# A fused cross-attention and feed-forward kernel: the eight accumulation banks shared out anew, with new engine orders

## The chip, the core and the metric

The kernel runs on one core of a Trainium2 chip. The metric is the device time in microseconds (us) of one execution. The core has five engines that run side by side and signal each other through semaphores: TensorE (PE) multiplies matrices and writes into PSUM, which has eight banks of 512 fp32 numbers per partition; VectorE (DVE) and ScalarE (ACT) read PSUM and on-chip memory; GpSimd (POOL) works on on-chip memory; SyncE (SP) issues the transfers (DMA).

## The reference

For 64 sequences of 64 rows and 256 columns, with a context of the same shape and a mask, four residual steps are taken (`LN` is a layer norm without weights):

```python
x = x + xattn(LN(x), ctx)      # 8 heads of 8 channels over 256 positions: q, k, v projections, rotary, softmax
x = x + bit_ffn(LN(x))         # activations rounded to 8 bits, ternary weights, hidden 1024, silu(gate) * val
x = x + cross(LN(x), ctx, mask)  # softmax(x ctx^T / 16, masked) ctx
x = x + tern_ffn(x)            # ternary weights by groups of 64, silu(gate) * up, RMS norm, down
```

In the first attention a sequence's 64 channels are the 8 heads of 8 channels each, and its 256 columns are the positions that attend to each other.

## The kernel before

Two sequences make a pair, there are 32 pairs, and a pair has 16 (sequence, head) units. Each unit has a 256 x 256 score matrix, and it is computed twice. **S** (line 435) puts queries on partitions, and DVE takes its row maxima (**mx**, line 871, 512 numbers per partition and unit). The 16 units' maxima are transposed on PE (**mxp**), copied (**mxc**) and written by a transfer (**md**) as an extra row beside the queries, so that the second product **T** (line 443), with keys on partitions, comes out with the maximum already taken off. ACT takes its exponential (**E**, line 591). **pv** (line 457, four per pair) multiplies by the values, and **u** copies the result out. S and T use 31 or 32 rows of PE's 128, a different quarter for each of four units in turn, so that up to four such products can run at once; pv uses 32 columns for each of four units.

All else is a chain of small steps per pair: `proj0 proj1 v` (projections), `r1 pc r2 rot hi lo kq` (rotary and its transfer), `sg rc d1 or ov om y x1` (normalising, output projection), then the first feed-forward network `bsB mvB rsB xnB amB sxB xr xq rq qT`, `Bg Bv` (gate and value products in two halves), `tB aB hB` (tanh on ACT, two products on DVE, each half), `amH sx hr hq ht Bd x2`; then the cross attention `xnD xcT xcTc sc wx pD pT pTc ro x3`; then the second network `xnC xh xl xT Cg Cu th aC hC hh hl hT Cd x4` and the store `st`.

The order of the work is written out by hand in `ORDER`: for each engine a list of steps, `name:shift`. All engines run the same loop of iterations, and in iteration `it` a step works on pair `it + shift`; so eight or more pairs are in flight at once. Each engine runs its list strictly in order and waits at each step for what it needs. Steps of the weight preparation (`c ab ra qa rn cl qb fx tn tc gm gv bs br fr ct val mn`) run once; their shifts are large numbers, which only place them in the first iterations.

PSUM is three tensors: `psS` with two banks for S, `psT` with two for T, `psW` with four for all other products. Unit n of S goes to bank n % 2 and waits until mx has read unit n - 2; T waits in the same way for E. For `psW` the table `BANKS` says which products share a bank, and `turn_before` finds for each product the one that held the bank before it; PE then waits for that one's reader (`READER`: aB1 for Bg1, hC0 for Cu0, aC1 for Cg1, pD for sc and so on). The waits of a step are in the branch of its kind, as here for the score products:

```python
after(pe, "mx", p, n - 2)      # S
after(pe, "E", p, n - 2)       # T
```

`BANK[...]` is used by the readers too (`tc gv r1 pc vst x1 tB aB hB x2 wx pD x3 aC hC x4` and others), so they follow a product to its bank without an edit.

## Time and profile before

| what | value |
|---|---|
| median of 3 runs | 884.59 us (882.81 to 884.67) |
| the profiled execution | 885.19 us, of which the span of instructions is 883.4 us |
| PE busy | 766.2 us, 87% of the span |
| DVE busy | 744.9 us, 84% |
| ACT busy | 688.0 us, 78% |
| POOL busy | 659.1 us, 75% |
| granted clock of PE, mean | 0.947 of full speed |

Busy time is the time in which an engine works on at least one instruction. Products overlap on PE and their ends are modelled, so the distance from the start of one step to the start of the next is the better measure of what a step costs there. A timeline line gives the start, the time taken, the engine, the line of the kernel, what is written from what, and how many instructions are merged in it; in square brackets stands how long the engine stood idle before and on what. In the waits, `A <- B` means that A waited for B.

### The profile page before, as it was taken

What the parts mean: (1) busy time and instruction counts of PE and PEld (TensorE: products, weight loads), DVE (VectorE), ACT (ScalarE), POOL (GpSimd) and SP (SyncE); (2) the same over time, 40 slices, a digit from 0 to 9 for tenths busy, and PEclk for the clock granted to TensorE, in tenths of its full rate; (3) what the DMA queues carried; (4) which work ended last, traced back from release to release, by engine and by line L of the source; (5) the groups of instructions that cost most, each with busy time, mean ns of one, the idle gap of its engine ahead of it and who ended that gap; (6) DMA issues with size and microseconds to landing.
All of it is one profiled execution on the core that took longest, in us unless ns stands there. A gap on an engine that the chain in (4) does not pass through costs nothing. (4 is left out here: it accounts for less than half of the span.)

```text
span 883.4 us, 21920 instructions
## 1 busy us (share of the span) xinstructions
PE 766.2 (87%) x6804; PEld 407.7 (46%) x6804; DVE 744.9 (84%) x1707; ACT 688.0 (78%) x1469; POOL 659.1 (75%) x1115
## 2 busy tenths in 40 slices
PE   0037878899999999999999999999999999998745
PEld 0023333444555555555555555555555554444422
DVE  0765778889999999999999999999999999966731
ACT  3655667779888888888888888888888889895531
POOL 5664435668888888888888888888888887677652
PEclk9995788889999999999999999999999999998986
DMA  9101122224444444444344444544444443345212
GB/s 338 11 13 55 38 64 57 78 72 103 104 109 108 104 109 104 101 114 103 101 101 104 107 109 109 110 107 105 109 109 105 104 102 98 90 85 108 68 46 71
DMA packets 210859, 84.67 MB, mean 96 GB/s; under 512 B 152748, under 2 KB 209708, under 8 KB 210744
## 3 DMA queue, kind: packets, MB, share of 16 engines
q1 hardware_dynamic: 210744, 83.28, 37.9%
q8 instruction: 55, 0.90, 0.4%
q14 instruction: 60, 0.49, 0.2%
HBM read 28.42 MB, written 4.72 MB: 38 GB/s over the span
## 5 line engine op out<-in xcount | busy, mean ns | idle before, releaser
L871 DVE TENSOR_REDUCE mx<-psS 128x2 f32<-128x512 f32 x512 | 338.2, 680 | 22.1 <-PE psS L435 21.4
L591 ACT ACTIVATE prob<-psT 128x512 f32<-128x512 f32 x512 | 293.8, 603 | 33.6 <-PE psT L443 32.6
L435 PE MATMUL psS<-KQ 31*128 31x256 f16 x1024 | 142.7, 283 | 23.5 <-DVE mx L871 21.5
L522 PE MATMUL psW<-guT,xT 128*128 128x512 bf16 x512 | 132.1, 393 | 15.8 <-DMA xT<-stage 13.1
L457 PE MATMUL psW<-prob,vst 128*32 128x256 f32 x2048 | 135.2, 394 | 0.1
L443 PE MATMUL psT<-KQ 32*128 32x256 f16 x1024 | 134.1, 278 | 1.0 <-ACT prob L591 0.5
L435 PEld LDWEIGHTS psS<-KQ 31*128 31x128 f16 x1024 | 42.1, 93 | 112.9 <-DVE mx L871 65.7
L777 POOL TENSOR_TENSOR stage<-stage 128x512 f16<-128x512 f32 x64 | 73.2, 1162 | 17.7 <-ACT stage L674 17.5
L457 PEld LDWEIGHTS psW<-prob,vst 128*32 128x32 f32 x2048 | 55.5, 111 | 60.5 <-issue 23.8
L484 PE MATMUL psW<-tern,xqT 128*128 128x512 bf16 x256 | 77.8, 386 | 4.0 <-DMA xqT<-xqB 3.6
L522 PEld LDWEIGHTS psW<-guT,xT 128*128 128x128 f16 x512 | 44.0, 100 | 76.9 <-issue 37.0
L601 ACT COPY uA<-psW 128x512 f32<-128x512 f32 x64 | 37.5, 586 | 53.2 <-PE psW L457 50.5
L763 POOL TENSOR_TENSOR hqB<-hrB,rnd 128x512 bf16<-128x512 f32 x64 | 66.5, 1041 | 15.4 <-ACT hrB L635 13.7
L531 PE MATMUL psW<-pT,stage 128*128 128x256 bf16 x512 | 66.2, 277 | 5.3 <-DMA stage<-stage 5.2
L757 POOL TENSOR_TENSOR r<-pc,tab 128x512 f32<-128x512 f32 x32 | 41.0, 1280 | 34.3 <-ACT pc L606 34.3
L970 DVE SCALAR_TENSOR_TENSOR stage<-stage,psW 128x512 f32<-128x512 f32 x64 | 43.7, 683 | 19.1 <-ACT stage L666 18.2
L531 PEld LDWEIGHTS psW<-pT,stage 128*128 128x128 f16 x512 | 50.7, 99 | 18.8 <-issue 5.5
L470 PE MATMUL psW<-cP,wsm 128*128 128x256 f32 x128 | 49.8, 474 | 5.5 <-POOL xnP L738 5.3
L978 DVE SCALAR_TENSOR_TENSOR stage<-stage,hsc,psW 128x512 f32<-128x512 f32 x64 | 47.5, 742 | 6.3 <-PE psW L522 5.7
L666 ACT ACTIVATE stage<-psW 128x512 f32<-128x512 f32 x64 | 39.6, 619 | 16.9 <-PE psW L522 16.9
L487 PE MATMUL psW<-brow,xqT 128*128 128x512 bf16 x128 | 49.1, 384 | 0.0
L635 ACT ACTIVATE hrB<-hB,sB 128x512 f32<-128x512 f32 x64 | 48.0, 754 | 0.6 <-DVE sB L939 0.6
(163 smaller groups left out, 1772.8 us busy)
## 6 DMA issues: line engine op xcount, KB each, us to landing
KQ<-hl SPq DMA_DIRECT2D x192, 64.0 KB, 2.0
xP<-in_x SPq DMA_DIRECT2D x32, 128.0 KB, 2.2
cP<-in_ctx SPq DMA_DIRECT2D x32, 128.0 KB, 2.2
xA<-in_x SPq DMA_DIRECT2D x32, 128.0 KB, 2.5
oV<-uA SPq DMA_DIRECT2D x32, 128.0 KB, 2.2
oR<-rden_d SPq DMA_DIRECT2D x128, 32.0 KB
cB<-in_ctx SPq DMA_DIRECT2D x32, 128.0 KB, 2.3
out<-x SPq DMA_DIRECT2D x32, 128.0 KB, 1.8
```

The costliest lines, as they stand in the source:

```text
L435: m = nc.tensor.matmul(psS[:, n % 2, T * k:T * k + T], KQ[p % DEEP][r, 1, g, 128 * k:128 * k + 128], KQ[p % DEEP][r, 0, g, :], start=True, ...
L443: m = nc.tensor.matmul(psT[:, n % 2, T * k:T * k + T], KQ[p % DEEP][r, 0, g, 128 * k:128 * k + 128], KQ[p % DEEP][r, 1, g, :], start=True, ...
L457: m = nc.tensor.matmul(bank[32 * j:32 * j + 32, :], vst[p % DEEP][:, k, 4 * n + j, :], prob[:, (4 * n + j) % 8, k, :], start=(k == 0), sto ...
L470: m = nc.tensor.matmul(bank[:, T * f:T * f + T], wqk[:, j, :], (cP, xnP)[f][:], start=True, stop=True)
L484: nc.tensor.matmul(bank, xqT[:, k, :], (gT if kind == "Bg" else vT)[:, k, 512 * n:512 * n + 512], start=(k == 0), stop=False)
L487: m = nc.tensor.matmul(bank, xqT[:, NK, :], brow[:, int(kind == "Bv"), 512 * n:512 * n + 512], start=False, stop=True)
L522: m = nc.tensor.matmul(bank, xT[:, NK * part + k, :], w[:, k, :], start=(k == 0 and part == 0), stop=(k == NK - 1 and part == 1))
L531: m = nc.tensor.matmul(psW[:, BANK["Cd0"], 0:T], hT[:, 8 * part + c, :], pT[:, c, :], start=(c == 0 and part == 0), stop=(c == 7 and part ...
L591: m = nc.scalar.activation(flat(prob[:, n % 8, :, :]), psT[:, n % 2, :], ACT.Exp, scale=float(HC) ** -0.5)
L763: m = nc.gpsimd.tensor_tensor(hqB[:, h], hrB[:, h], rnd[:].broadcast_to([P, 512]), ALU.subtract)
L777: m = nc.gpsimd.tensor_tensor(hhl[:, 1, n, :], hC[:, n, :], hhl[:, 0, n, :], ALU.subtract)
L871: m = nc.vector.tensor_reduce(mx[:, p % 2, :, 4 * (n % 4) + n // 4], psS[:, n % 2, :].rearrange("p (c s) -> p c s", c=NK), AX.X, ALU.max)
```

## The change

`psT` gets three banks and `psW` three; `psS` keeps two. T of unit n goes to bank (16 p + n) % 3 and waits for the exponential three units back, and E reads from that bank. `BANKS` has three lists in place of four. The five engine orders are new. No step is added or taken away. Some readings of the new lists: between mx1 and mx2 DVE has `rc aC0 sx hC0 wx amB`; PE has S14 and S15 between pv2 and pv3; Bg1 stands behind pv3, just ahead of Bv1 and mxp; T0, T1, T2 come directly after each other.

```diff
--- before.py
+++ after.py
@@ -68,27 +68,26 @@
 DEEP = 3
 SET_POOL = 2 * DEEP + 11
 ORDER = {
-    "pe": """S8:0 T6:-1 T7:-1 ro:-5 pv0:-1 S9:0 S10:0 T8:-1 tn2:15 proj0:2 pv1:-1 S11:0 T9:-1 T10:-1 S12:0 proj1:2
-           tn3:4 Bd:-4 T11:-1 S13:0 tn4:1 S14:0 T12:-1 Bg0:-3 Bg1:-3 S15:0 T13:-1 T14:-1 y:-2 Bv0:-3 gm:25 mxp:0
-           Bv1:-3 S0:1 S1:1 T15:-1 pv2:-1 pv3:-1 v:2 S2:1 T0:0 tn0:31 S3:1 T1:0 tn1:19 Cg0:-5 xcT:-4 S4:1 T2:0 S5:1
-           T3:0 Cg1:-5 tn5:-3 Cu0:-5 sc:-4 S6:1 T4:0 T5:0 S7:1 Cu1:-5 Cd0:-6 pT:-4 Cd1:-6""",
-    "dve": """rs:-5 mx7:0 x4:-7 mx8:0 x3:-5 bsC:-5 ra0:44 mx9:0 mvC:-5 bsP:3 mx10:0 mvP:3 r1:2 bs:6 mx11:0 mx12:0 x2:-4
-           bsD:-4 mx13:0 fx0:26 mx14:0 mvD:-4 ra2:32 mx15:0 ra1:35 aB0:-3 ct0:1 val:-1 aB1:-3 bsB:-2 hB0:-3 mvB:-2
-           hB1:-3 mx0:1 mx1:1 amH:-3 mx2:1 fx2:2 sx:-3 mx3:1 aC0:-5 cl2:4 mx4:1 cl1:21 amB:-2 cl0:31 gv:8 fx1:3
-           ct1:0 mx5:1 rc:-1 ct2:-1 hC0:-5 wx:-4 sxB:-2 aC1:-5 mx6:1 hC1:-5""",
-    "act": """pTc:-5 xr:-3 hh1:-6 ab2:20 rn0:24 tc5:-4 E6:-1 E7:-1 xq:-3 sq0:-6 fr0:13 tc2:6 c0:37 E8:-1 u0:-1 E9:-1
-           E10:-1 pc:2 c1:28 E11:-1 tc4:1 E12:-1 mn:0 xh:-5 tB0:-3 tB1:-3 x1:-2 ab1:22 tc0:16 E13:-1 mxc:0 rn2:20
-           E14:-1 E15:-1 sq1:-6 hi:2 u1:-1 vst:2 E0:0 E1:0 th0:-5 xcTc:-4 tc1:8 E2:0 fr1:2 fr2:1 hr0:-3 E3:0 hr1:-3
-           c2:26 ab0:25 th1:-5 E4:0 pD:-4 hh0:-5 tc3:3 E5:0 rn1:22""",
-    "pool": """rq:-3 qa2:8 qb2:2 qa1:26 lo:1 hl0:-6 hl1:-6 rsC:-5 xb:-3 xnC:-5 om:-2 qa0:63 qb1:3 r2:2 xl:-5 rsD:-4
-           rot:2 xnD:-4 rsB:-2 qb0:24 rsP:3 xnB:-2 ms:-6 xnP:3 hq0:-3 hq1:-3""",
-    "sp": """xP:4 ht:-3 or:-1 qT:-2 kq:2 cB:-3 br:111 xT:-4 md:1 hT:-5 xA:0 sg:0 cP:4 ov:0 d1:0 st:-6""",
+    "pe": """xcT:-5 T0:-1 T1:-1 T2:-1 Cu0:-6 sc:-5 S2:0 T3:-1 T4:-1 v:1 Cg1:-6 S3:0 T5:-1 T6:-1 S4:0 Cu1:-6 Cd0:-7
+           S5:0 T7:-1 T8:-1 tn5:2 S6:0 pT:-5 Cd1:-7 pv0:-1 S7:0 S8:0 T9:-1 tn1:35 tn0:39 T10:-1 tn4:9 ro:-5 pv1:-1
+           tn2:32 T11:-1 S9:0 T12:-1 S10:0 y:-2 Bd:-4 S11:0 T13:-1 proj0:2 Bg0:-3 S12:0 T14:-1 T15:-1 S13:0 Bv0:-3
+           pv2:-1 gm:45 S14:0 tn3:13 S15:0 pv3:-1 Bg1:-3 Bv1:-3 mxp:0 S0:1 S1:1 proj1:2 Cg0:-5""",
+    "dve": """mx1:0 rc:-2 aC0:-6 sx:-4 bs:16 fx0:25 fx2:2 val:7 cl0:31 hC0:-6 wx:-5 amB:-3 mx2:0 sxB:-3 mx3:0 mx4:0
+           cl1:20 aC1:-6 rs:-5 hC1:-6 ra2:29 mx5:0 mx6:0 x4:-7 bsP:3 mx7:0 mx8:0 x3:-5 bsC:-5 ct2:-3 gv:27 mvP:3
+           mvC:-5 mx9:0 mx10:0 x2:-4 mx11:0 bsD:-4 bsB:-2 ct0:1 r1:2 mvD:-4 fx1:5 mx12:0 mx13:0 aB0:-3 mvB:-2 ra0:53
+           hB0:-3 mx14:0 cl2:7 mx15:0 aB1:-3 hB1:-3 ct1:0 mx0:1 amH:-3 ra1:33""",
+    "act": """th0:-6 xcTc:-5 E0:-1 E1:-1 E2:-1 hr0:-4 E3:-1 pD:-5 vst:1 E4:-1 th1:-6 E5:-1 hr1:-4 hh0:-6 ab1:22 pTc:-5
+           c0:77 rn1:10 E6:-1 E7:-1 rn2:7 xr:-3 E8:-1 E9:-1 hi:1 fr2:0 xq:-3 E10:-1 u0:-1 E11:-1 x1:-2 E12:-1 hh1:-6
+           E13:-1 tc2:2 xh:-5 tc3:2 ab0:40 tc5:0 tB0:-3 mn:9 E14:-1 E15:-1 rn0:25 u1:-1 tB1:-3 ab2:21 mxc:0 tc0:8
+           sq0:-6 c1:64 tc4:2 fr0:1 c2:44 tc1:4 fr1:1 sq1:-6 pc:2""",
+    "pool": """xnP:2 ms:-7 qa0:96 r2:1 hq0:-4 qb1:21 rot:1 qa2:25 qb2:15 hq1:-4 rq:-3 hl0:-6 om:-2 lo:1 rsC:-5 xnC:-5
+           qb0:26 rsP:3 xl:-5 rsD:-4 hl1:-6 qa1:38 xnD:-4 rsB:-2 xb:-2 xnB:-2""",
+    "sp": """xP:3 or:-2 ht:-4 cB:-4 cP:2 qT:-3 kq:1 xT:-5 br:115 sg:-1 st:-8 md:0 hT:-6 d1:-1 xA:-1 ov:-1""",
 }
 
-BANKS = ("tn2 proj0 tn4 Bg1 gm pv2 xcT sc pT",
-         "proj1 Bg0 mxp v tn0 tn5 Cu0 Cd0",
-         "pv0 tn3 y Bv1 Cg1",
-         "ro Bd Bv0 tn1 Cg0 Cu1")
+BANKS = ("v Cd0 y proj0 pv2 mxp Cg0",
+         "xcT sc Cu1 tn5 ro Bd Bv0 gm tn3 Bv1",
+         "Cu0 Cg1 pT pv0 tn1 tn0 tn4 tn2 Bg0 Bg1 proj1")
 BANK = {name: bank for bank, names in enumerate(BANKS) for name in names.split()}
 
 READER = {**{f"tn{n}": f"tc{n}" for n in range(6)}, "gm": "gv", "proj0": "r1", "proj1": "pc", "v": "vst", "mxp": "mxc", "pv0": "u0", "pv2": "u1", "y": "x1", 
@@ -164,8 +163,8 @@
 
 
         psS = stack.enter_context(nc.psum_tensor("psS", [P, 2, 512], F32))
-        psT = stack.enter_context(nc.psum_tensor("psT", [P, 2, 512], F32))
-        psW = stack.enter_context(nc.psum_tensor("psW", [P, 4, 512], F32))
+        psT = stack.enter_context(nc.psum_tensor("psT", [P, 3, 512], F32))
+        psW = stack.enter_context(nc.psum_tensor("psW", [P, 3, 512], F32))
 
 
         tab = sb("tab", [P, 2 * T + P])
@@ -438,9 +437,9 @@
                     elif kind == "T":
                         if n == 0:
                             after_dma(pe, "md", p)
-                        after(pe, "E", p, n - 2)
+                        after(pe, "E", p, n - 3)
                         for k in range(NK):
-                            m = nc.tensor.matmul(psT[:, n % 2, T * k:T * k + T],
+                            m = nc.tensor.matmul(psT[:, (NH * p + n) % 3, T * k:T * k + T],
                                                  KQ[p % DEEP][r, 0, g, 128 * k:128 * k + 128],
                                                  KQ[p % DEEP][r, 1, g, :], start=True, stop=True)
                     elif kind == "mxp":
@@ -588,7 +587,7 @@
                             after(act, "pv", p, n // 4 - 2)
                         if n == 0 and p == 0:
                             after(act, "c", 0, 2)
-                        m = nc.scalar.activation(flat(prob[:, n % 8, :, :]), psT[:, n % 2, :], ACT.Exp,
+                        m = nc.scalar.activation(flat(prob[:, n % 8, :, :]), psT[:, (NH * p + n) % 3, :], ACT.Exp,
                                                  scale=float(HC) ** -0.5)
                     elif kind == "mxc":
                         after(act, "mxp", p)
```

## Rows read from the trace of the kernel before

**Rows 1.** Busy us (instructions) of PE, PEld, DVE, ACT, POOL; clock, DMA share, GB/s

```profile
400.00:600.00 200.00, 197.42 (x1881) 107.50 (x1880) 194.13 (x460) 176.72 (x399) 171.89 (x300) 1.00 0.44 106
```

**Rows 2.** Line 877, the reciprocal `rc`, from 190 to 745 us

```profile
L877 DVE RECIPROCAL rden<-den x25: 340/341/353, 197.7 to 739.6; 128x32 f32<-128x32 f32 x25
```

**Rows 3.** Waits from 300 to 700 us: total, times, longest

```profile
PEld psS L435 <- DVE mx L871: 25.5, 53, 0.6
...
DVE x L946 <- PE psW L492: 6.3, 17, 0.4
```

**Rows 4.** PE in order of time, one pair of the steady part

```profile
499.86 0.70 PE L470 MATMUL psW<-cP,wsm 128*128 128x256 f32 x2
...
500.83 1.04 PE L492 MATMUL psW<-tern,hqT 128*128 128x256 bf16 x8
501.80 0.28 PE L443 MATMUL psT<-KQ 32*128 32x256 f16 x1
...
502.14 0.60 PE L484 MATMUL psW<-tern,xqT 128*128 128x512 bf16 x2
...
502.79 0.59 PE L484 MATMUL psW<-tern,xqT 128*128 128x512 bf16 x2
...
503.87 0.70 PE L462 MATMUL psW<-oTA,wsm 128*128 128x256 f32 x2
...
504.83 0.59 PE L484 MATMUL psW<-tern,xqT 128*128 128x512 bf16 x2
...
506.77 1.93 PE L457 MATMUL psW<-prob,vst 128*32 128x256 f32 x32
...
514.73 1.04 PE L522 MATMUL psW<-guT,xT 128*128 128x512 bf16 x4
...
517.55 0.28 PE L435 MATMUL psS<-KQ 31*128 31x256 f16 x1
...
517.88 0.70 PE L513 MATMUL psW<-cB,pTD 128*128 128x256 f32 x2
518.51 1.07 PE L457 MATMUL psW<-prob,vst 128*32 128x256 f32 x16
...
521.09 1.07 PE L457 MATMUL psW<-prob,vst 128*32 128x256 f32 x16
522.09 0.28 PE L435 MATMUL psS<-KQ 31*128 31x256 f16 x1
```

**Rows 5.** ACT, then DVE, in order of time: `tB` and `aB` without other work

```profile
827.89 1.26 ACT L630 ACTIVATE stage<-psW,sB 128x512 f32<-128x512 f32 x2
...
828.60 1.28 DVE L923 SCALAR_TENSOR_TENSOR aB<-stage,psW 128x512 f32<-128x512 f32 x2 [2.29 <-ACT stage L630]
```

**Rows 6.** DVE in order of time, one pair of the steady part

```profile
499.86 0.48 DVE L897 SCALAR_TENSOR_TENSOR r<-psW,small,tab 128x256 f32<-128x256 f32 x1
500.25 1.28 DVE L871 TENSOR_REDUCE mx<-psS 128x2 f32<-128x512 f32 x2
501.90 0.48 DVE L946 SCALAR_TENSOR_TENSOR x<-psW,sB,x1b 128x256 f32<-128x256 f32 x1 [0.37 <-PE psW L492]
...
506.83 0.65 DVE L930 TENSOR_TENSOR hB<-aB,psW 128x512 f32<-128x512 f32 x1
507.40 1.28 DVE L871 TENSOR_REDUCE mx<-psS 128x2 f32<-128x512 f32 x2
...
515.16 0.15 DVE L914 TENSOR_SCALAR sB<-sB 128x1 f32<-128x1 f32 x1
```

**Rows 7.** POOL and PE at the start, PE at the end, a transfer

```profile
57.19 3.61 POOL L717 TENSOR_TENSOR tq<-tq,gsc 128x2048 bf16<-128x2048 bf16 x1
...
73.91 0.61 PE L435 MATMUL psS<-KQ 31*128 31x256 f16 x4 [1.66 <-DMA KQ<-hl]
...
864.01 5.94 PE L522 MATMUL psW<-guT,xT 128*128 128x512 bf16 x16 [7.46 <-DMA xT<-stage]
...
stage<-stage SPq DMA_TRANSPOSE x32, 3.8
```

## The prediction

> **What bounds the kernel now.** I read the stretches of the whole run first, then the spacing of one instruction that runs once per pair, then the waits, then one pair of the steady part in order of time on the VectorE (DVE) and the TensorE (PE). Between 400 and 600 us, at a granted clock of 1.00, PE is busy 197.4 and DVE 194.1 of 200 us, ScalarE (ACT) 176.7 and GpSimd (POOL) 171.9 [rows 1]. Both of the first two are nearly full. The reciprocal `rc` runs once per pair; its 25 runs from 197.7 to 739.6 are (739.6 - 197.7)/24 = 22.58 us apart [rows 2]. That is the steady period. In 400 us of it DVE waits only in front of `x2`, 6.3 us in 17 waits, 0.37 each; so DVE's own work is 22.58 - 0.37 = 22.21 us per pair, and no order of steps can go below that. PE's weight loads wait 25.5 us for the maxima (`mx`), 1.4 us per pair [rows 3]. So DVE bounds, and PE has little over a microsecond to spare.
>
> Why does PE cost what it costs? Scores S and T use one quarter of the array's rows each, and up to four of them run at once: a group of two S and two T takes 501.80 to 502.14, 0.34 us [rows 4]. So the price of a pair of scores is per group, not per product, and grouping matters. All else uses the full array, except `pv`, which uses quarters of its columns. Changing between these three ways of using the array costs something. `Bg0`, three products of 512 columns, takes 502.14 to 502.79, 0.65, so 256 columns take 0.108; `Bd`, eight of those and then a group, takes 0.97, which is 0.1 more than 8 x 0.108. `ro`, two fp32 products, takes 0.63 to `pv0`, where `y`, four of them with no change behind, takes 0.96, so 0.48 for two [rows 4]: 0.15 to 0.2 before a `pv`.
>
> **The change, part by part.** No instruction is added or removed; banks, waits on banks, and all five orders change.
>
> The third bank for T: a T now waits for the E three before, not two. The waits of PE's weight loads hold none of T on ACT; T never waited for a bank. I cost this at 0. It allows groups such as T0 T1 T2 in one go. ACT's work is the same and has some 2.6 us of idle time per pair, 22.58 x (1 - 176.7/200).
>
> PE's groups and changes of kind. Reading the old order in a circle there are 9 groups of scores and 21 stretches of one kind per pair; in the new one 10 groups and 24 stretches, because `pv2 pv3` is split by S14 S15, and S0 S1 stand alone. One group more is 0.34, three changes are 0.1 to 0.2 each: PE's work rises by 0.6 to 0.9 per pair, against the spare time of 1.4. By itself that would still fit. By the Trainium skill, TensorEngine Tiling (Array Packing), section Key Properties, changing the tiling mode drains the TensorE; if only this counted, the three drains would make 0.3 to 0.6 us per pair and 893 to 900 us in all. My sum is not made by that sentence.
>
> What decides is where the work stands. S has two banks, so S(n) waits for mx(n-2). In the new order DVE does `rc aC0 sx hC0 wx amB` between mx1 and mx2, and S4 waits for mx2. From there PE has, up to `Bg1`, all of this:
> - S4 by itself, since S3 T5 T6 can go before it: 0.34.
> - Cu1, Cd0, pT, Cd1: 514.73 to 517.55 = 2.82 [rows 4], plus 0.1 because S5 now stands between Cd0 and pT, plus 0.1 because a `pv` follows: 3.02.
> - pv0 1.00 (like pv1, 521.09 to 522.09); ro and pv1 0.63 + 1.00; together 2.63.
> - y 0.96 and Bd 0.97: 1.93. proj0 0.97 (499.86 to 500.83) and Bg0 0.65 + 0.1 before a group: 1.72.
> - Bv0 0.65 + 0.2 before a `pv`, pv2 1.00: 1.85. pv3 1.00 and Bg1 0.65: 1.65. (pv2 and pv3 together are 1.93 now.)
> - six groups of scores in between: 6 x 0.34 = 2.04.
>
> All of these are in [rows 4]. Sum: 0.34 + 3.02 + 2.63 + 1.93 + 1.72 + 1.85 + 1.65 + 2.04 = 15.18 us. In front 0.1 for mx2 to S4. Behind, `aB1` waits for `tB1`, which waits for `Bg1`: 0.2 until the last product has drained, 0.64 for the tanh (two take 1.26), 0.06 to DVE: 0.9 [rows 5]. Then DVE goes from aB1 to the end of mx2. From mx0 at 507.40 to sxB at 515.16 it does in 7.76 us six maxima and exactly `amH sx aC0 amB rc hC0 wx` [rows 6]; the new stretch has three maxima fewer (3 x 0.60), and aB1 (0.60, as long as a maximum: two of either take 1.28) and hB1 (0.57, 506.83 to 507.40, and 0.1 since it now stands right behind aB1) more: 7.76 - 1.80 + 1.27 = 7.23 us. Round the circle: 0.1 + 15.18 + 0.9 + 7.23 = 23.41 us. The same said from DVE: between mx2 and aB1 it has 22.21 - 7.23 = 14.98 of work, PE and ACT need 16.18, so it stands idle 1.2 us per pair where it now stands 0.37. I expect about 0.3 of it in front of `x2` (now after mx10, with S10, y and Bd to be done between mx8 and it) and the rest in front of `aB1`.
>
> The same reckoning on the kernel before goes from mx10 to S12, proj1, Bd and x2: 0.1 + 0.34 + 0.97 + 0.97 + 0.1 = 2.5, against r1 (two halves of 0.39, 499.86 to 500.25), the short mvP and two maxima of 0.60, some 2.1 of DVE's work, and gives the 0.4 that the row of x2 shows [rows 6]. So I trust it to some 0.1 for each two microseconds of PE work, less where pieces average. Lower bound: none of the surcharges for changes of kind (0.6 in all): 22.8. Upper bound: 0.3 for a bank that comes late: 23.7. I take 23.3, near the sum.
>
> psW with three banks: the close ones are proj1, which now follows Bg1 in its bank and so waits for aB1; Cg1, which follows Cu0 and waits for hC0; pT, which waits for aC1; Cu1, which waits for pD. Behind proj1 are Cg0, xcT and T0 to T2, behind Cg1 only S3, T5, T6; what is lost there (some 0.3 and 0.1) is taken out of the wait of S4 for mx2, which is about 0.5. I cost them at 0; without that cover they are 0.4 per pair. SP: `md` now lies between mxp and T0 with proj1, Cg0, xcT (2.4) in between, as before with pv2 pv3 v; `ht` waits for hq1 and behind it are cB and qT. I cost these at 0, up to 0.5 per pair if hr1 on ACT comes late.
>
> How often? 24 spacings are at 22.58 and about one more beside them: 25 x (23.3 - 22.58) = 18.0 us.
>
> **Start.** POOL's third `qb` (3.6 us) stood behind the first pair's layer norm, at 57.19 [rows 7]; now it is ahead of it, as is DVE's `fx2`. But it stood ahead of r2, rot and lo of pair 0 in both orders, and the first S waits for their transfer until 73.91 [rows 7]. So only the waits count: xnP of pair 0 comes some 5 us later, the second xP with it, and rsP, xnP of pair 1 still stand ahead of r2. I take +3; bounds 0 and +8.
>
> **End.** The last pair's Cg and Cu run as 16 products in 5.94 us from 864.01 [rows 7]. Now Cg1 must wait until hC0 has read Cu0's bank: two of four products leave the overlap, +1. hl1 moves behind xl on POOL, which shortens a circle that is level with another: 0. Bounds -4 and +3.
>
> **Sum**, on the profiled execution: 885.2 us (its span is 883.4; the median shown is 0.6 lower): 885.2 + 18.0 + 3 + 1 = 907.2, forecast 907.
>
> **Rivals.**
> - PE's stretch is shorter than I add up, say by 0.8: then DVE's own work and the wait at x2 set the pace as now, 22.58. For it: PE reads as busy 98.7% while its weight loads are free half the time, so its pieces may overlap more than starts show. Against: starts are differences between instructions in order, nothing overlaps them. 885 + 4 = 889.
> - Faster: the new order keeps DVE fed and even x2's wait goes. The floor is 22.21: 25 x (-0.37) = -9, and the start comes out level: 876 to 880, 878. It decides if PE reaches aB1's tanh within 14.98 us of mx2, for which my sum would have to be 1.2 too long, 8%. The notes point that way: the Trainium skill, Trainium Kernel Development and Optimization, section Best Practices, says steady bubbles can mean that PSUM ran out, and a third bank is there for T. But the waits are those of S for mx, and S keeps two.
> - Much slower: hr1, hq1, ht, Bd and x2 become a chain of their own, from hr1 being behind E4, th1, E5 on ACT. That chain has about 5.5 us from hr1's end until PE is ready for Bd, and hq and a transposing transfer to fit into it (the longest one on the page lands after 3.8) [rows 7]. If it decides, 0.5 more per pair: 920 and more.
>
> **How the numbers follow.** Forecast (a period of 22.9 to 23.6) 0.70, with a range of its own of 895 to 917; level 0.08; faster 0.10; much slower 0.12. The range 890 to 919 leaves out the faster one and most of the much slower one. A measurement tells 0.2%, 1.8 us, from no change. Faster by more than that 0.11, within it 0.05, slower 0.84.
>
> **What would show it.** The spacing of `rc` at 23.3; DVE waiting in front of aB1 for ACT's tanh, 0.7 or more once per pair, and in front of x2; PE's waits for mx in one place, S4. If aB1 does not wait, the sum over PE's stretch is wrong. If T0 waits for the transfer of the maxima, or proj1 for aB1 with nothing regained at S4, the cover is wrong. The first S after 75 and the last x4's distance from the last rc show start and end.

## The result and the profile after

The changed kernel takes 937.95 us (median of 4 runs, 933.39 to 940.11) against 884.63 for the kernel before beside it: a ratio of 1.0601 (95% interval 1.0555 to 1.0647). The sign of the forecast was right, its size was not: 907 was forecast, with 890 to 919 as the range, and the time lies 19 us above the upper end. The profiled execution takes 936.18 us, its span is 934.4, which is 51.0 more than before.

Where the 51.0 us lie I read from two instructions. The first row maximum starts at 81.2 instead of 74.6 us, and from the last one to the end of the span it is 110.8 instead of 110.9: so the start costs 6.6, the end nothing, and 44.5 lie between. From the fifth to the 29th reciprocal `rc`, the same 24 spacings as in [rows 2], it is now 573.6 instead of 541.9 us: 31.7. The other 12.8 lie in the first pairs and in the last ones.

The reciprocal, now line 876, from 190 to 785 us (durations in ns, then first and last start):

```profile
L876 DVE RECIPROCAL rden<-den x25: 340/342/345, 207.7 to 781.3; 128x32 f32<-128x32 f32 x25
```

That is a mean of 23.90 us; most single spacings are 23.8. The stretch from 400 to 600 us, in the columns of [rows 1]:

```profile
400.00:600.00 200.00, 190.07 (x1750) 100.81 (x1777) 190.47 (x441) 170.68 (x381) 161.84 (x282) 1.00 0.42 101
```

No engine is as full as before, at the same granted clock of 1.00: PE falls from 197.4 to 190.1 and DVE from 194.1 to 190.5. So neither bounds by its work alone; a circle of waits does. (Here a circle means a chain of waits through several engines that comes back to its own start one pair later, so that its length is the spacing.) The waits from 300 to 700 us (total, times, longest; a wait under 0.15 us is in no such list), those of DVE and then of PE:

```profile
DVE aB L922 <- ACT stage L629: 11.2, 17, 0.8
DVE x L945 <- PE psW L491: 2.8, 16, 0.2
...
PE psW L469 <- DVE aB L922: 5.2, 17, 0.3
PE psW L521 <- DVE stage L977: 3.5, 16, 0.2
PE psW L509 <- DVE stage L969: 3.4, 17, 0.2
...
PE psS L434 <- DVE mx L870: 2.7, 16, 0.2
...
PEld psS L434 <- DVE mx L870: 21.2, 66, 0.5
```

DVE stands idle in front of `aB1` once per pair, 0.66 us each, where it did not wait at all before, and in front of `x2` 0.17 instead of 0.37 [rows 3]. PE's products wait at four places: `proj1` for aB1, Cg1 for `hC0`, `pT` for `aC1`, S4 for mx2. The first three are waits for a bank of `psW`. The weight loads (PEld), which run beside the products, wait for a maximum at four places per pair and not at S4 alone.

The circle itself, on PE from S4 (498.43) to Bv1 (513.86); `tB1` starts when Bg1's last product (line 486) has drained:

```profile
498.43 0.39 PE L434 MATMUL psS<-KQ 31*128 31x256 f16 x2 [0.17 <-DVE mx L870]
498.75 1.04 PE L521 MATMUL psW<-guT,xT 128*128 128x512 bf16 x4
499.62 1.04 PE L530 MATMUL psW<-pT,stage 128*128 128x256 bf16 x8
...
501.20 0.33 PE L509 MATMUL psW<-tab,pD 128*128 128x128 f32 x1 [0.20 <-DVE stage L969]
...
512.20 1.07 PE L456 MATMUL psW<-prob,vst 128*32 128x256 f32 x16
513.43 0.38 PE L483 MATMUL psW<-tern,xqT 128*128 128x512 bf16 x1 [0.16 <-issue]
513.65 0.38 PE L486 MATMUL psW<-brow,xqT 128*128 128x512 bf16 x1
513.86 0.59 PE L483 MATMUL psW<-tern,xqT 128*128 128x512 bf16 x2
...
515.52 0.70 PE L469 MATMUL psW<-cP,wsm 128*128 128x256 f32 x2 [0.30 <-DVE aB L922]
```

and on DVE from the `aB1` that waits to the mx2 which releases the next S4 (521.51 + 0.69), with that pair's line 915, of which more below:

```profile
514.78 0.69 DVE L922 SCALAR_TENSOR_TENSOR aB<-stage,psW 128x512 f32<-128x512 f32 x1 [0.69 <-ACT stage L629]
515.50 0.69 DVE L929 TENSOR_TENSOR hB<-aB,psW 128x512 f32<-128x512 f32 x1
...
521.51 0.69 DVE L870 TENSOR_REDUCE mx<-psS 128x2 f32<-128x512 f32 x1
...
522.42 0.70 DVE L915 SCALAR_TENSOR_TENSOR sB<-sB,gam_q 128x1 f32<-128x1 f32 x1
```

So: 0.06 from mx2 to S4; S4 to Bv1 513.86 - 498.43 = 15.43; Bv1's start to aB1's 514.78 - 513.86 = 0.92; aB1 to the end of mx2 522.20 - 514.78 = 7.42. Together 23.83. The circle of the forecast is there, in the place it named, with 15.18 + 0.9 + 7.23 + 0.1 = 23.41 on paper. The difference of 0.42 needed the experiments.

**One instruction had grown.** Between mx2 and mx3 stands `sxB`, four operations on one column. The third of them multiplies two tensors and a scalar; no step was added or taken away, yet its duration is different. First before (line 916), whole run, then after (line 915), from 300 to 700 us; ns as shortest, median, longest:

```profile
L916 DVE SCALAR_TENSOR_TENSOR sB<-sB,gam_q x32: 208/210/893, 131.6 to 820.2; 128x1 f32<-128x1 f32 x32
```

```profile
L915 DVE SCALAR_TENSOR_TENSOR sB<-sB,gam_q x17: 693/697/703, 308.0 to 689.2; 128x1 f32<-128x1 f32 x17
```

What goes on beside it, after, in order of time:

```profile
498.60 0.69 DVE L915 SCALAR_TENSOR_TENSOR sB<-sB,gam_q 128x1 f32<-128x1 f32 x1
499.21 0.15 DVE L917 RECIPROCAL sB<-sB 128x1 f32<-128x1 f32 x1
...
498.00 1.27 POOL L768 TENSOR_TENSOR rot<-r 128x512 f32<-128x512 f32 x1
```

It ends when POOL's `rot` ends (498.00 + 1.27 = 499.27), and does so within 0.02 us in all 23 pairs between 190 and 750 us. In the kernel before, POOL at that moment stood idle in front of `rq`, which waits for this same `sxB`:

```profile
515.82 0.19 POOL L743 CAST xqB<-sB 128x3 bf16<-128x3 f32 x1 [0.62 <-DVE sB L918]
```

That the price exists could have been read before: one of the 32 took 0.893, and the last one 0.69, at 820.23, while POOL's `hq` ran from 818.87 to 820.91. I had looked at the median.

### The profile page after: what moved, and what is told of

It is laid out like the page before. It is cut to its first block, busy times and chain, and to the rows that moved or that the text cites. A ratio compares the mean times of both kernels' runs of the same rounds, so it can differ in the third digit from the quotient of the medians.

```text
span 934.4 us, 21831 instructions
## 1 busy us (share of the span) xinstructions
PE 780.3 (84%) x6714; PEld 403.9 (43%) x6804; DVE 768.1 (82%) x1707; ACT 695.3 (74%) x1469; POOL 657.8 (70%) x1115
## 4 chain that ended last, share of the span: by engine, by line
PE 44%; DVE 27%; issue 11%; POOL 6%; DMA 5%; ACT 4%; SPq 2%; DVEq 0%; POOLq 0%; ACTq 0%
PE psW L456 14%; DVE mx L870 8%; PE psS L434 6%; DVE sB L905 5%; PE psW L483 4%; PE psW L469 4%; DVE stage L969 3%; PE psW L530 3%; PE psW L491 2%; DVE aB L922 2%; ACT stage L629 2%; PE psW L486 2%; PE psW L461 2%; PE psW L512 2%; PE psT L442 2%
## 5 line engine op out<-in xcount | busy, mean ns | idle before, releaser
L870 DVE TENSOR_REDUCE mx<-psS 128x2 f32<-128x512 f32 x512 | 331.9, 680 | 34.3 <-PE psS L434 32.2
L590 ACT ACTIVATE prob<-psT 128x512 f32<-128x512 f32 x512 | 288.7, 603 | 19.9 <-PE psW L456 16.1
L434 PE MATMUL psS<-KQ 31*128 31x256 f16 x1024 | 140.9, 286 | 17.5 <-DVE mx L870 11.4
L456 PE MATMUL psW<-prob,vst 128*32 128x256 f32 x2048 | 144.9, 403 | 2.0 <-DVE r L896 1.3
L442 PE MATMUL psT<-KQ 32*128 32x256 f16 x1024 | 111.5, 285 | 5.5 <-DMA KQ<-mxs 3.2
L776 POOL TENSOR_TENSOR stage<-stage 128x512 f16<-128x512 f32 x64 | 74.2, 1159 | 14.4 <-ACT stage L673 14.4
L530 PE MATMUL psW<-pT,stage 128*128 128x256 bf16 x512 | 68.3, 280 | 4.8 <-DMA stage<-stage 4.8
L483 PE MATMUL psW<-tern,xqT 128*128 128x512 bf16 x195 | 63.4, 382 | 10.3 <-issue 5.3
L629 ACT ACTIVATE stage<-psW,sB 128x512 f32<-128x512 f32 x64 | 44.0, 688 | 27.8 <-PE psW L486 23.6
L922 DVE SCALAR_TENSOR_TENSOR aB<-stage,psW 128x512 f32<-128x512 f32 x64 | 43.7, 683 | 24.6 <-ACT stage L629 24.6
L969 DVE SCALAR_TENSOR_TENSOR stage<-stage,psW 128x512 f32<-128x512 f32 x64 | 41.9, 654 | 21.8 <-ACT stage L665 21.8
L469 PE MATMUL psW<-cP,wsm 128*128 128x256 f32 x128 | 47.6, 456 | 12.3 <-DVE aB L922 8.3
L772 POOL TENSOR_TENSOR hl<-rot,hl 128x512 f16<-128x512 f32 x32 | 37.5, 1173 | 26.4 <-ACT hl L615 26.4
```

Source lines behind the costliest of these rows:

```text
L434: m = nc.tensor.matmul(psS[:, n % 2, T * k:T * k + T], KQ[p % DEEP][r, 1, g, 128 * k:128 * k + 128], KQ[p % DEEP][r, 0, g, :], start=True, ...
L442: m = nc.tensor.matmul(psT[:, (NH * p + n) % 3, T * k:T * k + T], KQ[p % DEEP][r, 0, g, 128 * k:128 * k + 128], KQ[p % DEEP][r, 1, g, :], ...
L456: m = nc.tensor.matmul(bank[32 * j:32 * j + 32, :], vst[p % DEEP][:, k, 4 * n + j, :], prob[:, (4 * n + j) % 8, k, :], start=(k == 0), sto ...
L469: m = nc.tensor.matmul(bank[:, T * f:T * f + T], wqk[:, j, :], (cP, xnP)[f][:], start=True, stop=True)
L483: nc.tensor.matmul(bank, xqT[:, k, :], (gT if kind == "Bg" else vT)[:, k, 512 * n:512 * n + 512], start=(k == 0), stop=False)
L530: m = nc.tensor.matmul(psW[:, BANK["Cd0"], 0:T], hT[:, 8 * part + c, :], pT[:, c, :], start=(c == 0 and part == 0), stop=(c == 7 and part ...
```

## The experiments

All compute the whole result. A letter and number name each kernel: a changes the kernel after, b the kernel before, o mixes the two. "Spacing" is the mean from the fifth to the 29th `rc`: before 22.58, after 23.90. Ratios are to the kernel before, with the 95% interval.

**a1: the grown instruction without its second tensor.** `tensor_scalar` takes both factors as per-partition scalars.

```diff
-                        nc.vector.scalar_tensor_tensor(out=sc[:, 5:6], in0=sc[:, 1:2], scalar=sc[:, 1:2],
-                                                       in1=gam_q[:, 1:2], op0=ALU.mult, op1=ALU.mult)
+                        nc.vector.tensor_scalar(sc[:, 5:6], sc[:, 1:2], sc[:, 1:2], gam_q[:, 1:2], ALU.mult, ALU.mult)
```

> The changed kernel, with the third instruction of sxB (line 915) written as a tensor_scalar with two scalar operands instead of a scalar_tensor_tensor; the values are the same. In the changed kernel that one-column instruction takes 0.70 us where it took 0.21 before, and it runs while POOL is inside rot. Theory A (the instruction waits for POOL's, and what counts is only that aC1 comes late and pT waits for it, 0.28 per pair): the instruction falls to 0.15 to 0.22, the spacing of rc from 23.83 to 23.55, the time by about 9 us, to some 929 us. Theory B (DVE's whole work sets the pace): the spacing falls by all of 0.49, the time by 15 us, to 922. Theory C (that form is slow there for another reason than its form): nothing changes, 938.

926.5 us, ratio 1.0485 (1.0439 to 1.053), spacing 23.52, most single ones 23.4: theory A. The instruction takes 0.265 us, beside the same work of POOL:

```profile
L915 DVE TENSOR_SCALAR sB<-sB,gam_q x17: 264/266/266, 305.7 to 681.3; 128x1 f32<-128x1 f32 x17
```

The wait in front of aB1 stays (11.4 us in 17), so a circle still sets the pace, but the spacing is shorter by 0.38, nearly all of the 0.43 that the instruction lost. Yet the instruction stands behind mx2 and ahead of aB1, in the part where DVE has time to spare. PE, from S4 to Bv1, shows why:

```profile
516.87 0.39 PE L434 MATMUL psS<-KQ 31*128 31x256 f16 x2 [0.17 <-DVE mx L870]
517.19 1.04 PE L521 MATMUL psW<-guT,xT 128*128 128x512 bf16 x4
518.06 1.04 PE L530 MATMUL psW<-pT,stage 128*128 128x256 bf16 x8
519.37 0.33 PE L509 MATMUL psW<-tab,pD 128*128 128x128 f32 x1
```

From Cd0 to pT it is now 519.37 - 518.06 = 1.31, where it was 501.20 - 499.62 = 1.58, and pT no longer waits. There are two circles: one through mx2 and S4, and one through sxB, mx3, mx4, aC1 and pT, which joins it on PE. The second one was the longer; pT is on it because it shares a bank with Cg1, whose reader is aC1. Without it the circle is 0.06 + 15.10 + 0.92 + 7.42 = 23.50 in the profile of a1 (15.10: the pair ahead has its S4 at 493.37, and its Bv1 at 508.47). That is my sum, 23.41, within 0.1.

**a3: amB behind mx2.** This shortens the circle through S4 by amB's 0.4 and not the one through pT.

```diff
-hC0:-6 wx:-5 amB:-3 mx2:0 sxB:-3
+hC0:-6 wx:-5 mx2:0 amB:-3 sxB:-3
```

> The changed kernel, with amB behind mx2 on DVE instead of ahead of it, so that mx2 ends 0.45 us earlier and S4 can go in one group with S3, T5 and T6. Theory A (there are two circles of equal length, one through mx2 and S4 and one through aC1 and pT, and this shortens only the first): the spacing stays at 23.75 to 23.83, the wait of pT for aC1 grows from 0.2 to 0.6, the time stays within 3 us of 938. Theory B (the circle through S4 alone, as the prediction had it): the spacing falls by 0.45, the time by 14 us, to 924.

935.84 us, ratio 1.0591 (1.0566 to 1.0616), spacing 23.93. PE's wait of S4 for mx is gone from its list and the wait of pT for aC1 is still 3.5 us in 17. So the circle through S4 was not alone, and shortening it alone buys nothing: theory A, though pT's wait did not grow to 0.6. Besides, the weight loads of S6, in the group just ahead of pT, wait 0.28 for mx4 (at 499.54 us), which stands behind sxB too. No run gives pT a bank of its own under this order, so how much of the second circle is the shared bank and how much is mx4 was not separated.

**a2 and a2b: Bg1 ahead of pv3**, which takes pv3's 1.2 us out of the way to tB1. In a2 only PE's order changes, in a2b ACT's too.

```diff
-           pv2:-1 gm:45 S14:0 tn3:13 S15:0 pv3:-1 Bg1:-3 Bv1:-3 mxp:0
+           pv2:-1 gm:45 S14:0 tn3:13 S15:0 Bg1:-3 pv3:-1 Bv1:-3 mxp:0
```

```diff
-rn0:25 u1:-1 tB1:-3
+rn0:25 tB1:-3 u1:-1
```

> The changed kernel, with Bg1 one place earlier on PE, ahead of pv3. Theory A (the circle S4, Bg1, tB1, aB1, mx2 sets the pace, and PE has 22.65 us of work without waits): aB1's wait of 0.66 is gone, the spacing falls to between 23.0 and 23.3, the time by 16 to 25 us, to some 917. Theory B (PE is full: three more changes of kind and one more group of scores set the pace, and aB1's wait is only where it shows): the spacing stays above 23.6 and the wait moves to another step, 932 or more.

954.26 us, ratio 1.0794 (1.0755 to 1.0833), spacing 24.40: slower than the change itself. ACT and DVE:

```profile
619.53 0.58 ACT L600 COPY uA<-psW 128x512 f32<-128x512 f32 x1 [2.62 <-PE psW L456]
620.01 0.69 ACT L629 ACTIVATE stage<-psW,sB 128x512 f32<-128x512 f32 x1
...
620.74 0.69 DVE L922 SCALAR_TENSOR_TENSOR aB<-stage,psW 128x512 f32<-128x512 f32 x1 [1.23 <-ACT stage L629]
```

`u1`, which waits for pv3, stands ahead of tB1 on ACT, so the product that comes earlier is read later. I had moved a step on one engine without its reader's queue. The spacing lies in theory B's band, but for this reason and not because PE is full.

> The changed kernel with Bg1 ahead of pv3 on PE and, on ACT, tB1 ahead of u1. In the run before this one Bg1 alone was moved; ACT's list has u1, which waits for pv3, ahead of tB1, so tB1 came later, aB1's wait grew from 0.66 to 1.23 and the spacing from 23.83 to 24.40. Theory A (aB1 is on the circle that sets the pace): with tB1 free, aB1's wait of 0.66 goes, the spacing falls to 23.0 to 23.3 (DVE has 23.0 of its own there), the time to 910 to 920. Theory B (PE is full): 23.6 or more, 930 or more.

932.63 us, ratio 1.0555 (1.0539 to 1.057), spacing 23.80. The wait in front of aB1 is gone, and still only 5 us come back. DVE and POOL:

```profile
497.96 1.09 DVE L915 SCALAR_TENSOR_TENSOR sB<-sB,gam_q 128x1 f32<-128x1 f32 x1
...
497.76 1.27 POOL L768 TENSOR_TENSOR rot<-r 128x512 f32<-128x512 f32 x1
```

Now the instruction comes 0.2 us behind rot's start and stands for 1.09 us until rot ends (499.03). DVE is earlier, POOL is not, and most of the gain is given back in one column of work. None of the readings above had this; it is theory B's number again, and again not its cause.

**a12b: a1 and a2b together.**

> The same, and with sxB's third instruction as a tensor_scalar (it took 0.49 us less in an earlier run, DVE's own work 22.5). Theory A: the spacing falls to 22.6 to 22.9, the time to 897 to 908. Theory B (PE's own work with its added changes of kind, some 22.7, and its bank waits are the next bound): 23.0 to 23.3, no lower than the run without it.

915.5 us, ratio 1.0359 (1.0333 to 1.0385), spacing 23.13, most single ones 22.9. Alone the two save 11 and 5 us, together 22: each had been masked by the other. With both, DVE waits 0.35 a pair in front of x2, 0.2 between two of its own steps, and nowhere else in more than 2 pairs; in most pairs its own work sets the pace again. The time is still above theory A's 897 to 908.

**a123b and a125: a12b with more.** a123b adds a3; a125 adds the start of the next experiment.

> The changed kernel with the tensor_scalar in sxB, Bg1 ahead of pv3, tB1 ahead of u1, and amB behind mx2. Theory A (at 22.9 DVE sets the pace with its own work of about 22.4 and the waits of x2 and hB1, and the wait of S4 for mx2 is no longer on the circle): 22.9, 915. Theory B (the circle mx2, S4, Bd, x2 is what is left): x2's wait of 0.35 goes, 22.5 per pair, 904.

> The changed kernel with four repairs together: the tensor_scalar in sxB, Bg1 ahead of pv3, tB1 ahead of u1, and the later weight steps. The first three gave 22.9 per pair and 915.5 us. Theory A (the pieces add): 911 to 914, still some 3% above the kernel before, of which 22.9 against 22.58 per pair makes 10 us and the first ten pairs, start and end the rest. Theory B (they overlap): 915 or more.

917.9 (ratio 1.0389, 1.0364 to 1.0414) and 917.29 (1.0365, 1.0333 to 1.0397), spacings 23.26 and 23.20: nothing beyond a12b. About half of the 24 single spacings are 22.9 in both, and 9 or 10 are 23.4 or more (6 in a12b). In all three PE waits in 5 or 6 of 17 pairs for the transposing transfer of `Bd`'s input, up to 0.6:

```profile
PE psW L491 <- DMA hqT<-hqB: 2.3, 6, 0.6
```

This is a125. It is the chain of the prediction's much slower rival, hr, hq, ht, Bd, x2; it surfaces only once the circle is shorter. That these waits make the longer spacings is likely, and was not tried.

**a5: the start as before.** The preparation steps of `after` are given smaller shifts, so that POOL's third `qb` stands again behind the first layer norm.

```diff
-... tn5:2 ... tn4:9          (pe)
+... tn5:0 ... tn4:1
-... fx2:2 ...                (dve)
+... fx2:1 ...
-... tc4:2 ...                (act)
+... tc4:1 ...
-... qb2:15 ...               (pool)
+... qb2:2 ...
```

> The changed kernel with the weight preparation's last steps placed later: qb2 behind the first pair's xnP, fx2, tn4, tc4 and tn5 one or two iterations later. The first maximum stands at 81.2 us in the changed kernel and at 74.6 before; the stretch from the first to the last maximum is 742.4 against 697.9. Theory A (the start's 6.6 us are a piece of their own, from qb2 standing ahead of the first layer norm): the first maximum comes at 77 to 79, the stretch behind it stays within 1 us of 742.4, the time falls by 2 to 4 us. Theory B (a later first pair also made the next ones wait, and explains the 6 us that the stretch has beyond 31 times 1.24): the stretch gets shorter by 3 us or more as well.

933.13 us, ratio 1.0561 (1.0532 to 1.059), an interval that overlaps that of the kernel after. In the profiled execution, a5's longest, the span is 934.7 against 934.4: the first maximum does come 3.9 us earlier, at 77.3, but the first `rc` is at 118.8 as in the kernel after (118.6). POOL, in the kernel after and then in a5:

```profile
54.55 4.52 POOL L716 TENSOR_TENSOR tq<-tq,gsc 128x2048 bf16<-128x2048 bf16 x1 [3.74 <-DVE tq L834]
...
83.34 0.61 POOL L737 TENSOR_TENSOR xnP<-ceP,rsP 128x256 f32<-128x256 f32 x1 [7.33 <-PE psW L469]
```

```profile
79.45 0.61 POOL L737 TENSOR_TENSOR xnP<-ceP,rsP 128x256 f32<-128x256 f32 x1 [6.54 <-PE psW L469]
```

`xnP` of the pair two ahead now stands first in POOL's list, waits for proj0 to have read its buffer, and `r2 rot lo` of the next pair are queued behind it. Their transfer goes out at 88.71 after, 84.82 in a5 and 78.31 before. The lists were made for the steady part; in the first pairs each in-order wait shows. Why a5 loses its 3.9 us again by the first rc stays open; the granted clock between 77 and 119 us is 0.54 there, against 0.62 in the kernel after and 0.68 before.

What the later `qb` does change is this (DVE's second step of `fx1`, after and then a5):

```profile
55.64 4.51 DVE L838 TENSOR_TENSOR wb<-wb,tq 128x2048 bf16<-128x2048 bf16 x1
```

```profile
55.61 1.22 DVE L838 TENSOR_TENSOR wb<-wb,tq 128x2048 bf16<-128x2048 bf16 x1
```

In the kernel after it ends 1.1 us behind qb's end (59.07); without qb beside it, it takes 3.3 us less, and the first layer norm, which stands behind it on DVE, comes at 56.75 instead of 60.08. Those 3.3 us are most of the 3.9.

**b2 and b3: the contention brought into the kernel before.** `rq` is moved behind `hl0` on POOL, so that POOL works while sxB runs; b3 has the two-scalar form of a1 as well.

```diff
-    "pool": """rq:-3 qa2:8 qb2:2 qa1:26 lo:1 hl0:-6 hl1:-6
+    "pool": """qa2:8 qb2:2 qa1:26 lo:1 hl0:-6 rq:-3 hl1:-6
```

> The kernel before, with rq on POOL moved between hl0 and hl1, so that POOL is inside hl0 when DVE comes to the third instruction of sxB (line 916 there), where now it stands idle, waiting for sxB. Theory A (a scalar_tensor_tensor of DVE whose operands lie in on-chip memory waits until POOL's running instruction ends): line 916 rises from 0.21 us to between 0.5 and 1.1, DVE's own work by as much, the spacing of rc from 22.58 to 23.0 to 23.4, the time to 895 to 910. Theory B (it is slow in the changed kernel for its neighbours on DVE): it stays at 0.21, the time at 884.

> The same, with that instruction as a tensor_scalar with two scalar operands. Theory A: it takes 0.27 us as in the changed kernel with the same edit, the spacing is 22.6 again, the time 884 to 887. Theory B: no different from the run without it.

b2: 897.95 us, ratio 1.0159 (1.0128 to 1.019), spacing 23.29. b3: 884.15 us, 0.9997 (0.9979 to 1.0015), spacing 22.63. The instruction from 300 to 700 us, in b2 and then in b3:

```profile
L916 DVE SCALAR_TENSOR_TENSOR sB<-sB,gam_q x17: 834/855/868, 316.3 to 688.1; 128x1 f32<-128x1 f32 x17
```

```profile
L916 DVE TENSOR_SCALAR sB<-sB,gam_q x18: 264/265/266, 310.7 to 695.7; 128x1 f32<-128x1 f32 x18
```

The same order on POOL costs 1.6% with one form of one instruction and nothing with the other. 0.855 - 0.210 = 0.65 per pair, and the spacing rises by 0.71: where DVE bounds, the whole of it is paid. Both came out as theory A has it, so this is shown and not only argued: only POOL's order was changed, and in b2 the instruction ends within 0.02 us of POOL's `hl0` in all 24 pairs between 190 and 750 us.

By the Trainium skill, SBUF — State Buffer, section Who interferes with whom, a DVE instruction with two inputs in SBUF (the on-chip memory) contends with a GpSimd instruction that reads SBUF, the lock is exclusive, and issue order decides who blocks. The rows agree: blocked to the end of POOL's instruction with two tensors (0.69 to 1.09 us), not blocked with one (0.265).

**o2, o3 and o1: banks and orders apart.** o2 has the old orders with three banks for T and three for psW; o3 the same with T's third bank taken back; o1 the new orders with two and four banks as before. The old orders need a table of their own for three banks. In o1 T8 had to move behind S7.

```diff
 o2, o3: all orders of before, and
+BANKS = ("Cg1 pT pv0 Bg0 Bv0 v tn0 tn2 tn4",
+         "Cg0 Cu0 Cu1 ro proj1 Bg1 Bv1 tn1 tn3 tn5",
+         "xcT sc Cd0 proj0 Bd y mxp pv2 gm")
 o3 and o1:
+        psT = stack.enter_context(nc.psum_tensor("psT", [P, 2, 512], F32))
+                        after(pe, "E", p, n - 2)
 o1: psW with 4 banks, T8 behind S7, and the third list of after split in two
+         "Cu0 pv0 tn1 tn0 tn4 tn2 Bg0 proj1",
+         "Cg1 pT Bg1")
```

> The orders of the kernel before with the new bank counts (three for T, three for the other products), and a sharing of the three fitted to the old orders. Theory A (the orders cost the time, not the counts): Cd0 waits for pD and Bv0 for aB0, about 0.5 each, of which PE has 1.4 to spare; the spacing stays within 22.6 to 23.1, 886 to 898. Theory B (three banks for the other products are too few under any order): 23.5 or more, 905 or more.

> The old orders with the three shared banks of the run o2, but T left with two banks, so that one bank is not used at all. Theory A (under the old orders all of o2's loss is from the three banks for the other products, and T's third bank brings nothing): the spacing is 23.5 as in o2, the time within 3 us of 910. Theory B (the third T bank won back a part): above 23.7, 915 or more.

> The new orders with the old bank counts: two for T (waiting for E two units back), four for the others, where Bg1, Cg1 and pT have the fourth; T8 had to go from the group of S5 to that of S7. Theory A (the third bank for T is what these orders lean on): T2, T6 and T10 stand in groups of three or behind E that has just begun, each costs PE 0.5 to 0.8, and the spacing rises to 24.5 or more, 955 or more. Theory B (the missing fourth bank costs more than the third T bank brings): proj1's 0.30, Cg1's 0.22 and pT's 0.2 go, the spacing falls to 23.3 to 23.6, some 925.

o2: 910.12 us, ratio 1.0302 (1.0281 to 1.0322). o3: 914.86, 1.0337 (1.0305 to 1.0369). The spacings are 23.47 and 23.48, the waits the same; those of o2, DVE first:

```profile
DVE x L945 <- PE psW L491: 10.6, 17, 0.6
...
PE psW L483 <- DVE aB L922: 6.0, 17, 0.4
PE psW L530 <- ACT pD L652: 5.7, 17, 0.3
PE psS L434 <- DVE mx L870: 5.4, 17, 0.3
```

The profiled executions differ by 0.9 us in span, and that lies in the first and last pairs; the medians lie 4.7 apart with overlapping intervals, and o3's profiled execution is its shortest, so whether the third bank is worth anything outside the steady part stays open. In the steady part of the old orders T's third bank changes nothing, and the bank that psW gives up for it costs 0.89 us per pair. Two waits were not there before: a product waits for aB1, another for pD, 0.35 each, and x2 waits 0.62 instead of 0.37 behind them. How the rest of the 0.89 comes about was not traced; part of it is waits too short for the list, 0.12 a pair in front of hB and 0.14 in front of the maxima. The table for three banks is mine, by hand; a better one may cost less.

o1: 1001.47 us, 1.1327 (1.1297 to 1.1357), spacing 25.65:

```profile
PE psT L443 <- ACT prob L591: 32.2, 48, 0.9
```

With two banks PE waits for E 2.0 us per pair in the new orders. These orders need the third bank; the old ones have no use for it in the steady part.

**b1, b4 and b5: is x2's wait of before worth anything?** b1 puts Bd ahead of proj1; b4 does too, exchanges the banks of Bg0 and Bg1 and puts mxp behind Bv1; b5 only moves bsP on DVE.

```diff
 b1, pe
-S12:0 proj1:2 tn3:4 Bd:-4
+S12:0 Bd:-4 proj1:2 tn3:4
 b4: b1 and
-y:-2 Bv0:-3 gm:25 mxp:0 Bv1:-3
+y:-2 Bv0:-3 gm:25 Bv1:-3 mxp:0
-BANKS = ("tn2 proj0 tn4 Bg1 ...", "proj1 Bg0 ...
+BANKS = ("tn2 proj0 tn4 Bg0 ...", "proj1 Bg1 ...
 b5, dve
-bsP:3 mx10:0 mvP:3 r1:2 bs:6 mx11:0
+mx10:0 bsP:3 r1:2 mvP:3 bs:6 mx11:0
```

> The kernel before, with Bd ahead of proj1 on PE, nothing else. Theory A (before, DVE sets the pace with 22.21 us of its own work and 0.37 of waiting for Bd): the wait of x2 is gone, the spacing of rc falls from 22.58 to 22.2 to 22.3, the time by 8 to 10 us, to some 875. Theory B (pc and r2 come 1 us later and POOL, which has under 2 us to spare per pair, or PE's bank waits take it back): the spacing stays at 22.5 or more, 883 to 890.

> The kernel before with Bd ahead of proj1, as in an earlier run that came out at 23.15 per pair because Bg0 waited 0.8 for pc in proj1's bank; now Bg0 has the bank of proj0 and Bg1 that of proj1, and Bv1 goes ahead of mxp, which shares Bg1's bank. Theory A (with the bank wait gone DVE's own 22.21 sets the pace): the spacing is 22.2 to 22.35, the time 873 to 879. Theory B (PE or the later mxp takes it back): 22.6 or more, 884 or more.

> The kernel before with bsP (0.31 us) from ahead of mx10 to behind it on DVE, so that S12, proj1 and Bd begin 0.31 earlier in DVE's order and the same work lies in front of x2. Theory A (x2's wait of 0.37 is the whole distance between DVE's work of 22.21 and the spacing of 22.58, and nothing else is late by as much): the wait falls to under 0.1, the spacing to 22.25 to 22.35, the time by 6 to 9 us, to some 877. Theory B (as when Bd was moved, PE, which has as little to spare, gives the wait back in front of a maximum): 22.5 or more, 883 to 886.

b1: 895.72 us, ratio 1.0136 (1.0112 to 1.016), spacing 23.15. b4: 898.23, 1.0156 (1.0127 to 1.0184), spacing 23.10. In both the wait of x2 is gone and another has come; b1 and then b4:

```profile
DVE mx L871 <- PE psS L435: 15.8, 18, 0.9
...
PE psW L484 <- ACT pc L606: 14.7, 18, 0.8
```

```profile
DVE mx L871 <- PE psS L435: 12.3, 35, 0.5
```

In b1 Bg0 waits in proj1's bank for pc, 0.8 a pair. In b4 that wait is absent, PE waits only 0.3 a pair for mx, and DVE waits 0.7 a pair for S: one step moved on PE turns the bound from DVE to PE. That shows how little room [rows 1] left. Both had been expected to be faster than the kernel before (theory A, some 875). b5: 881.68 us, 0.9981 (0.9968 to 0.9994), spacing 22.56, x2's wait as before (5.9 us in 17). It is the fastest kernel of the study, by 0.2%, and not by the wait I meant it to shorten: its first rc comes at 111.1 instead of 112.2, while theory A asked for 877 through a shorter spacing.

## Why the prediction was wrong in its size

Step by step, in its own terms.

- **What bounds.** DVE with 22.21 of own work, PE close behind: right for the kernel before. But "little over a microsecond to spare" was read from the waits of the weight loads, which run beside the products; the products themselves idle 5.8 us in 18 waits, 0.3 a pair, and b1 and b4 lost 0.5 a pair by moving one step on PE.
- **The place.** S4 behind mx2, aB1 waiting "0.7 or more", x2 waiting less: right. aB1 waits 0.66, and the only products that wait for mx are those of S4.
- **The sum over PE's stretch**, 15.18: 15.10 in a1, 15.43 in the kernel after. The sizes of the pieces, the surcharges for changing from quarters to the full array, and the price per group hold. The 0.33 too little are pT: 0.20 that it waits and what the group ahead of it loses.
- **psW with three banks at 0: this step failed.** I named "pT, which waits for aC1" and covered it with S4's wait for mx2. But pT stands behind S4, and what is lost behind a wait isn't taken out of it: from Cd0 to pT 0.27 is lost (1.58 against 1.31 in a1). proj1's wait for aB1 (0.30) was covered, as said; it is ahead of the S4 of the next circle, which still waits 0.17. The text had 0.4 per pair for the case without cover, and a1 gives back 0.38, but that the two are close is luck: the 0.4 was made of proj1's and Cg1's waits, which stayed covered.
- **DVE's durations taken as fixed: this step failed too.** I moved sxB past POOL's steps in time without asking what POOL does beside it. The 0.49 that line 915 grew is what makes aC1 late. Both errors meet in one place: a bank shared with a reader behind a stretched instruction. Nor was 22.21 a fixed amount of work: less the listed waits, DVE takes some 23.0 of the 23.9 per pair. Of the 0.8 more, 0.49 is line 915; the rest is in small pieces where steps have other neighbours (from start to next start, 0.13 more for `aB`, 0.12 for `amB`), and no run takes them apart.
- **DVE from aB1 to mx2**, 7.23: 7.33, taken as there from aB1's start to the start of sxB (514.78 to 522.11). The 7.42 above goes to the end of mx2, which overlaps sxB's start by 0.09; from sxB's start to S4 it is 0.14, where 0.1 was put down. From aB1's start to hB1's it is 0.72, not 0.70, and from hB1's to mx0's 0.61, not 0.57; the rest is hundredths.
- **23.3 chosen though the sum was 23.41.** No reason for going below was given, and there was none: 0.1 per pair.
- **Number of pairs.** 25 spacings at 1.32 more each would be 33.0, against 18.0. The steady part misses 31.7 - 24 x 0.72 = 14.4 us.
- **First and last pairs, costed at one spacing in all:** 12.8 - 0.7 = 12.1 missed. From the first to the fifth rc it is 89.1 instead of 85.5; from the 29th to the last 66.9 instead of 60.3, spacings of 23.0, 23.1 and 20.8 instead of 21.3, 21.0 and 18.0. Most of the rest is rc's place: the last one comes 2.7 us sooner behind the last maximum than before. I had carried over the fall-off of the kernel before. It goes with the orders and not with what bounds the steady part: o2, with the old orders and more waits, falls from 23.5 to 21.8, 21.1 and 19.1, and a12b, with the new orders and DVE's work setting the pace, only from 22.9 to 22.1, 21.8 and 21.1. What in the new orders does it stays open.
- **Start**, +3 with 0 to 8: +6.6. `qb` took 4.52 instead of 3.61 us, DVE's `fx1` beside it 4.51 instead of 1.22, and the layer norm stands behind fx1: most of the 3.9 us that a5 takes back at the first maximum. That looks like the contention of sxB's kind, which the prediction did not ask about here either. xnP at the head of POOL's list is a wait that I had not put down. In a5's profiled execution nothing of the 3.9 is left by the first rc.
- **End**, +1: 0, from the last maximum on. By the distance that the prediction named, from the last rc to the last x4, it is 83.4 instead of 80.8, but that is again rc's place.
- **The rivals.** Level and faster: no. T's third bank as a gain: o2 against o3 shows none in the steady part of the old orders. The much slower one, 920 and more, was right in number and wrong in cause: its chain hr, hq, ht, Bd shows only in a12b, a123b and a125, in one pair of three. That a number over 920 came is no support for it.

Together 14.4 + 12.1 + 3.6 - 1 = 29.1 of the 29.0 by which the span missed its forecast (51.0 against 22.0).

Where did the change's loss come from, then? Three banks for psW, with my table, cost the old orders 26 us (o2) to 30 (o3). The new orders, with their own table, come out at 53: nothing of that is won back and about as much again is lost, of which a1 and a2b recover 22: the second tensor operand, and the way from pv3 to tB1. Since the two tables differ, this is a comparison and not a division of the loss. What is left in a12b, 31 us by its span of 914.2, is 6.5 at the first rc, 3.0 to the fifth, 13.3 in the steady part, and 7.9 behind it; the last two were not taken apart further.

## What to carry to other kernels

Before a step is moved, look at the longest duration of each instruction in the trace and not only at the median; where one is far above, look at what the other engine did beside it, since the same may become the rule. When a wait is covered by another, check that it stands ahead of the one that covers it in the queue, and look for every circle that passes through a stretch: taking away the longest shows only the next, and two repairs may be worth little alone and much together. A freed bank is worth the wait that it ends: look for that wait first, and price the waits that come where the bank is taken from.

## What the runs showed of the hardware

- A one-column `scalar_tensor_tensor` of 0.21 us takes 0.69 to 1.09 us where POOL is inside a `tensor_tensor` of 1.16 to 1.27 us on on-chip memory, and ends within 0.02 us of POOL's instruction in each of the 70 cases between 190 and 750 us in the kernel after, a2b and b2; as `tensor_scalar`, whose second factor is a per-partition scalar too, it takes 0.265 beside the same work. The lost time is in the instruction's duration and stands as busy, not as a wait; no list of waits shows it.
- `tensor_scalar` is not free of it as such. In the kernel before, a one-column one took 0.14 us and one of 64x16 took 1.44 us beside the same `qb`; the latter ended with it, and its twin behind it took 0.23:

```profile
49.11 0.14 DVE L850 TENSOR_SCALAR gam_q<-gam 128x1 f32<-128x1 f32 x1
49.38 1.44 DVE L858 TENSOR_SCALAR b16d<-b,rgam 64x16 f32<-64x16 f32 x1
50.84 0.23 DVE L859 TENSOR_SCALAR b16d<-b,rgam 64x16 f32<-64x16 f32 x1
...
47.19 3.61 POOL L717 TENSOR_TENSOR tq<-tq,gsc 128x2048 bf16<-128x2048 bf16 x1 [3.03 <-DVE tq L835]
```

- POOL's third `qb` took 4.52 us and DVE's `fx1` beside it 4.51 in the kernel after. In a5, where qb comes later, they took 3.61 and 1.22. This agrees with the same contention, each waiting for the other in turn; no run was made for it alone.
